# Seven formed heads instead of six in the projections of an attention kernel, with three reorderings of its DMA issues

## What is computed

```python
# attention, 32 heads of 128: INNER = 4096
q = rms_norm(xn @ Wq + bq, gq);  k = rms_norm(xn @ Wk + bk, gk);  v = xn @ Wv + bv
attn = softmax(einsum("bhqd,bhkd->bhqk", q, k) * 128 ** -0.5)
x = x + layernorm(einsum("bhqk,bhkd->bhqd", attn, v) @ Wo + bo)      # xn = layernorm(x)
# feed-forward: a base product, and 8 gated experts of rank 16
x = x + layernorm(xn @ W_base.T + b_base + moe(xn) * 2.0)            # xn = layernorm(x)
```

## Time and profile before

| | |
|---|---|
| plain runs, us | 1054.54 (1053.43 to 1057.06) |
| profiled execution, us | 1056.27 |
| its span, us | 1054.5 |
| TensorE busy | 1034.8 us, 98% |
| VectorE, ScalarE, GpSimd busy | 851.4, 781.6, 769.7 us |
| mean granted clock | 0.995 of full speed |

### The profile page before, as it was taken

One profiled execution on the slowest core, in us unless ns is written; L12 is line 12 of the kernel. 1 busy time (PEld: TensorE's weight loads), 2 busy tenths in 40 slices (PEclk: granted clock), 3 DMA queues, 4 the chain that ended last, 5 costly groups with the idle time before them and its releaser, 6 DMA issues.

```text
span 1054.5 us, 18881 instructions
## 1 busy us (share of the span) xinstructions
PE 1034.8 (98%) x5613; PEld 547.3 (52%) x5613; DVE 851.4 (81%) x1849; ACT 781.6 (74%) x1614; POOL 769.7 (73%) x715
## 2 busy tenths in 40 slices
PE   8999999999999999999999999999999999999997
PEld 5444444444434655556555555555555555555454
DVE  8887888788775788777887887788788788888887
ACT  4775767678876777775788788688787878878656
POOL 2799999977877477775777877778778778767313
PEclk9999999999999999999999999999999999999999
DMA  6789766677674779987777767967876886986812
GB/s 243 198 218 273 246 208 237 193 218 231 201 182 143 199 169 260 246 154 200 160 166 182 196 172 181 193 176 161 217 182 151 210 196 166 228 200 141 175 37 80
DMA packets 312772, 200.04 MB, mean 190 GB/s; under 512 B 275553, under 2 KB 279521, under 8 KB 312673
## 3 DMA queue, kind: packets, MB, share of 16 engines
q1 hardware_dynamic: 304752, 194.24, 71.0%
q10 hardware_dynamic: 7920, 4.62, 2.2%
HBM read 96.03 MB, written 35.68 MB: 125 GB/s over the span
## 4 chain that ended last, share of the span: by engine, by line
PE 88%; DVE 3%; ACT 3%; DMA 3%; issue 2%; POOL 1%; ACTq 0%; SPq 0%; POOLq 0%; DVEq 0%
PE ps L1852 25%; PE ps L1854 25%; PE ps L1853 25%; PE ps L2115 3%; PE ps L2116 3%; PE ps L2117 3%; DMA qk_top_scratch<-qk_top 2%; PE ps L1975 1%; PE ps L1977 1%; PE ps L1976 1%; DVE stats L2419 1%; ACT squares L1260 0%; DMA y<-x 0%; POOL otl L1046 0%; PE ps L2031 0%
## 5 line engine op out<-in xcount | busy, mean ns | idle before, releaser
L2943 DVE SCALAR_TENSOR_TENSOR pair_q<-ps,row_inv,pair_q 128x512 f16<-128x512 f32 x256 | 174.4, 744 | 50.5 <-ACT pair_q L1541 47.3
L1532 ACT ACTIVATE ps<-ps,neg_max 128x512 f32<-128x512 f32 x256 | 168.2, 657 | 51.7 <-DVE ps L2929 51.7
L2929 DVE TENSOR_SCALAR_CACHE_REDUCE ps<-ps,score_down 128x512 f32<-128x512 f32 x256 | 177.3, 756 | 17.4 <-PE ps L1854 16.7
L1541 ACT ACTIVATE pair_q<-ps,row_inv 128x512 f16<-128x512 f32 x256 | 154.4, 689 | 5.7 <-DVE row_inv L2936 5.6
L1852 PE MATMUL ps<-xh,wa_hi 128*128 128x512 f16 x416 | 158.3, 381 | 0.3 <-DVE wa_lo L2535 0.3
L1853 PE MATMUL ps<-xl,wa_hi 128*128 128x512 f16 x416 | 158.1, 380 | 0.0
L1854 PE MATMUL ps<-xh,wa_lo 128*128 128x512 f16 x416 | 158.1, 380 | 0.0
L1013 POOL TENSOR_TENSOR k_lo<-qk_in,k_hi 128x512 f16<-128x512 f32 x62 | 71.7, 1156 | 37.9 <-ACT k_hi L1489 37.8
L1852 PE MATMUL ps<-wo_hi,oth 128*128 128x512 f16 x256 | 97.1, 379 | 1.7 <-issue 0.9
L1852 PE MATMUL ps<-k_hi,qk_in 128*128 128x512 f16 x256 | 97.2, 380 | 1.0 <-issue 0.7
L1854 PE MATMUL ps<-wo_hi,otl 128*128 128x512 f16 x256 | 97.1, 379 | 0.0
(11 more groups left out here) (368 smaller groups left out, 2742.7 us busy)
## 6 DMA issues: line engine op xcount, KB each, us to landing
q_k_scratch<-qk_out SPq DMA_DIRECT2D x64, 512.0 KB, 4.3
qk_in<-q_k_scratch SPq DMA_DIRECT2D x64, 512.0 KB, 3.7
wa_stage<-w_qk SPq DMA_DIRECT2D x32, 512.0 KB, 6.1
u_stage<-w_vo SPq DMA_DIRECT2D x32, 512.0 KB, 7.3
wo_stage<-w_vo SPq DMA_DIRECT2D x16, 512.0 KB, 5.6
x_first<-w_vo SPq DMA_DIRECT2D x12, 512.0 KB, 4.7
qk_tops<-qk_top_scratch ACTq DMA_DIRECT2D x27, 128.0 KB, 5.1
pair_k<-pair_q SPq DMA_TRANSPOSE x130, 4.0
```

Source lines behind the costliest of these rows:

```text
L1532: act.activation(ps[:, SCORE + i, :], ps[:, SCORE + i, :], ACT.Exp, bias=neg_max[:, sl, i:i + 1], scale=-1.0, accum_out=row_sum[:, sl, i:i ...
L1541: act.activation(pair_q[:, 0, i, :], ps[:, SCORE + i, :], ACT.Identity, scale=row_inv[:, sl, i:i + 1]).then_inc(high_ready, 1)
L2929: dve.tensor_scalar(ps[:, SCORE + i, :], ps[:, SCORE + i, :], score_down[:, sl, i:i + 1], None, ALU.mult, ALU.min, accum_out=neg_max[:, sl ...
L2943: dve.scalar_tensor_tensor(out=pair_q[:, 1, i, :], in0=ps[:, SCORE + i, :], scalar=row_inv[:, sl, i:i + 1], in1=pair_q[:, 0, i, :], op0=AL ...
```

## The change

It does four things.
1. `FIRST` becomes 8: the odd head of pair 8 (head 17) is formed as well, seven heads in all. With it the four sums for the first formed head on GpSimd go from ahead of pair 8 to ahead of pair 7.
2. ScalarE's load of the tops for the next even head goes from ahead of the query of batch 1 to behind that query, the second copy into `K_BANK` and the rest of the query.
3. On SyncE the weights and the unit of the next pair's even head are issued ahead of the formed head's two stores.
4. `top_v` is reduced, stored and loaded ahead of and behind pairs 8 and 9, where it was pairs 12 and 13.

```diff
-        FIRST, LAST_PAIR = PAIRS // 2 + 1, PAIRS - 2
+        FIRST, LAST_PAIR = PAIRS // 2, PAIRS - 2
@@ SyncE, formed_pair
-                weights(h)
-                load_unit(h + 3, 1, h + 3)
+                if p == FIRST:
+                    weights(h)
+                    load_unit(h + 3, 1, h + 3)
                 weights(h + 1)
                 store_even(0)
                 if p < LAST_PAIR:
                     load_unit(h + 4, 0, h + 4)
                 store_even(1)
+                if p < LAST_PAIR:
+                    weights(h + 2)
+                    load_unit(h + 5, 1, h + 5)
                 sp.wait_ge(k_out_ready, 2 * h + 4)
                 sp.wait_ge(q_lo_ready, 4 * FIRST + 2 * f + 2)
                 for b in range(2):
                     sp.dma_start(q_k_scratch[h + 1:h + 2, b].rearrange("a p w n -> p (a w) n"),
                                  qk_out[:, 1, b]).then_inc(stored[1][b], 16)
-            for p in range(FIRST, LAST_PAIR - 1):
+            for p in range(FIRST, LAST_PAIR + 1):
                 formed_pair(p)
-            sp.wait_ge(v_top_ready, 1)
-            sp.dma_start(vo_top_scratch[0], top_v[:, :]).then_inc(v_top_stored, 16)
-            formed_pair(LAST_PAIR - 1)
-            sp.wait_ge(v_top_stored, 16)
-            sp.dma_start(tops_v[:, :], vo_top_scratch[0:1].broadcast_to([P, P])).then_inc(v_tops_loaded, 16)
-            formed_pair(LAST_PAIR)
+                if p == FIRST:
+                    sp.wait_ge(v_top_ready, 1)
+                    sp.dma_start(vo_top_scratch[0], top_v[:, :]).then_inc(v_top_stored, 16)
+                if p == FIRST + 1:
+                    sp.wait_ge(v_top_stored, 16)
+                    sp.dma_start(tops_v[:, :], vo_top_scratch[0:1].broadcast_to([P, P])).then_inc(v_tops_loaded, 16)
@@ ScalarE, formed_pair
                 square_key(0, 6)
-                if p < LAST_PAIR:
-                    load_tops(h + 4, 0)
                 act.wait_ge(acc_ready, 4 * h + 4)
                 even_query(1, 7)
                 act.wait_ge(k_out_ready, 2 * h + 2)
                 copy(K_BANK, 8)
                 even_rest(1, 4)
+                if p < LAST_PAIR:
+                    load_tops(h + 4, 0)
@@ VectorE
-            for p in range(FIRST, LAST_PAIR - 1):
-                formed_pair(p)
             largest_value()
-            formed_pair(LAST_PAIR - 1)
-            formed_pair(LAST_PAIR, value_scales)
+            for p in range(FIRST, LAST_PAIR + 1):
+                formed_pair(p, value_scales if p == LAST_PAIR else None)
```

## The result

The changed kernel takes 1059.17 us (median of 22 runs, 1053.28 to 1065.89), the kernel before 1055.91 in the same session (22 runs, 1053.43 to 1061.7). The ratio is 1.0027, 95% interval 1.0016 to 1.0038: 3 us slower, where 1051.0 and a gain were predicted, and outside the range of 1048.4 to 1055.2. The profiled execution took 1061.99 us, with a span of 1060.0 against 1054.5 of before. That is 5.5 us more, so it shows more of the loss than the median has.

The account below looks back on a forecast made before the run. It took TensorE, 98% busy, as the bound, plus a stall in pair 13. From the profiled 1056.27 us it took 1.3 for six matmuls and 4.1 for the stall, added 0.1 for late loads: 1051.0, range 1048.4 to 1055.2.

Parts of the forecast that it names:

- Step 4: Small store of top_v moves to pairs 8/9, its meeting with the tops' store into pair 9: 0, 2.0 us if late.
- the prediction's own deadline: Formed head's stores may land as late as 16.7 us into the next pair, whose formed key wants them.
- Step 2: Load of the tops behind ScalarE's copy: pair 13's stall goes, -4.1 us; the load's lateness costs 0, at most 1 us.
- the cover of 0.3 us: In pair 13 the copy could end at 300.0, against 300.36 when TensorE wants it.
- The stall itself: Before pair 13's last product TensorE stands still 2.36 us, then the slow clock costs 1.7: 4.1 us in all.
- Step 1: Head 17 formed: 48 matmuls of 512 columns become 42 on TensorE, 1.3 us less.
- Step 3: SyncE issues next weights and unit ahead of the formed head's stores, issued no later: 0, bounds -1 and +4 us.
- Step 5: GpSimd's four sums for head 17 ahead of pair 7 make it 3.4 to 4.3 us later: cost 0, at most 3.5.
- The stall moves to pair 9: Rival: the stall goes to pair 9 with the small store; 1053.0 to 1055.1 us, chance 0.14.
- Slower: Rival: formed head's stores land too late in many pairs behind 1 MB of loads; 10 us lost, 1061, chance 0.08.

Follow-up runs that it names:

- e: Changed kernel with the small store of top_v moved inside pair 8, between the even head's two stores; 1054.50 us, ratio 0.9988 to the kernel before.
- i: Kernel before with only the small store of top_v, its load and the reduction moved to around the first formed pairs (9, 10); ratio 1.0023.
- d: Changed kernel with FIRST back at 9, so six formed heads, and the small store behind pair 9; ratio 0.9994 to the kernel before.
- l: Changed kernel with six formed heads and the small store of top_v inside pair 9; ratio 0.9996 to the kernel before.
- f: Kernel before with only ScalarE's load of the tops moved behind the copy of the odd head; ratio 1.0002.
- a: Changed kernel with the small store of top_v, its load and VectorE's reduction back at their old places; ratio 1.0026 to the kernel before.
- o: Kernel before with only the small store of top_v moved into pair 13, between the even head's two stores; ratio 0.9965.
- g: Kernel before with seven formed heads and nothing else changed; ratio 0.9994.
- p: Kernel before with seven formed heads and the small store of top_v moved into pair 13; ratio 0.9966.
- h: Kernel before with only SyncE's next weights and unit issued ahead of the formed head's stores; ratio 0.9993.
- b: Changed kernel with SyncE's old order, the formed head's stores ahead of the next weights and unit; ratio 1.0016 to the kernel before.
- n: Changed kernel with SyncE's old order of stores and loads, and the small store of top_v inside pair 8; ratio 0.9980 to the kernel before.
- q: Changed kernel with the small store inside pair 8, and in pair 8 alone the next loads behind the formed head's stores; ratio 0.9968 to the kernel before.
- m: Changed kernel with the small store of top_v issued twice in a row behind pair 8; ratio 1.0036 to the kernel before.

## Why the prediction was wrong

- **Step 4 failed, and it decides.** "The bad meeting with the store of the tops moves with it, into pair 9. Early pairs lag less ... I take 0." The place was right, the price was not. In pair 9 of the changed kernel's profile the meeting costs 8.4 us of standstill and 1.6 of clock. Moved to a quiet place, the ratio falls from 1.0027 to 0.9988 (e); brought in alone, it is 1.0023 (i). The price also hangs on the seventh head, as d (0.9994) and l (0.9996) show: with six heads and the other parts of the change, the meeting costs plain runs nothing that is told apart.
- The lag of 4.7 us for the stores' issue was taken from pair 10 of before. In the changed kernel it was 8.0 us: GpSimd's low half that gates them ended 7.1 us into the pair (it waited 0.73 us for ScalarE and took 2.31 us for the first half in place of 1.15), and the issues that now stand in front added 0.9. By the prediction's own deadline, 16.7 us into the pair, that leaves 8.7 us for landings of 13. In e, where they go out 6.1 us into the pair, even 10.8 us were too long, and TensorE waited 0.89.
- **Step 2 failed as a sum.** "By this alone the stall goes: -4.1 us." f, with this part alone, measured 1.0002. The copy was in time for the last product of pair 13, as forecast. The term that was left out is the next one: the unit's load, issued behind the small store, landed after 12.1 us, and through VectorE it held the first formed product of pair 14 until 308.32, where it stood before (308.39). The prediction looked only at the key, the copy and the load of the tops, for which it took "0, at most 1 us". In a, where the unit's load has moved ahead, the stores hold pair 13 instead. The key itself was later than it assumed: 14.2 us behind the first formed product of its pair in f, 13.8 before, which used up the cover of 0.3 us, though TensorE did not wait for it there.
- **The stall itself was read right**: it is in plain runs, at about its full size in the session of o, which takes away its cause alone and gains 3.7 us (0.9965), against the 4.1 forecast for it.
- **Step 1 right in the profile, not measurable in the time**: 6 matmuls fewer, pair 8 at 19.4 us in g, ratio 0.9994; o and p do not differ.
- **Step 3 right alone within 0.2% (h, 0.9993), wrong in one point.** That the stores "are issued no later" overlooked that an issue can hold the queue: 3.64 us for one load of weights, of which 0.9 us reached the stores. Taking this part back in the changed kernel gained nothing that is told apart (b, 1.0016). Pairs 10 and 11 of the changed kernel keep 19.4 us with the loads in front.
- **Step 5: the four sums were sized right, the cost of being behind was not.** They took 3.3 us, but what followed slowed down too. GpSimd's timeline of the changed kernel in pairs 7 and 8, and then an instruction of VectorE:

```profile
174.21 1.26 POOL L907 TENSOR_TENSOR w_sum<-wa_stage 128x512 f32<-128x512 f32 x1
175.44 2.09 POOL L912 TENSOR_TENSOR w_sum<-wa_stage 128x256 f32<-128x256 f32 x3
...
181.51 2.42 POOL L823 TENSOR_TENSOR qk_out<-q_s,qk_out 128x512 f16<-128x512 f32 x1
...
192.12 3.41 POOL L832 TENSOR_TENSOR acc<-acc,squares 128x512 f32<-128x512 f32 x2
195.51 1.15 POOL L849 TENSOR_TENSOR xs<-qk_in,xs 128x512 f16<-128x512 f32 x1
```

```profile
180.35 2.56 DVE L2551 SCALAR_TENSOR_TENSOR w_form_a<-w_sum,qk_up,w_form_a 128x1280 f16<-128x1280 f32 x1
```

  The last form of x starts 11.1 us into pair 8, where the earlier trace rows has 188.45 - 183.8 = 4.7: 6.5 us later, not 3.4 to 4.3. An instruction of 1.15 us took 2.42 beside VectorE's of 2.56, which took 1.54 at 205.33. The Trainium skill's rule on the shared port ("SBUF — State Buffer", Who interferes with whom) agrees in kind, and the prediction applied it to the four sums and not to what they push into VectorE's work. ScalarE's key square waited 1.43 us for it. In g a backlog of the same sums alone costs TensorE nothing; how much of the formed head's late stores comes of it in company is not shown.
- **The rivals.** Two were half right. "The stall moves to pair 9" had the place and priced it by the old standstill. "Slower" had the mechanism, stores that land later than the room left for them, and spread it over many pairs where it struck one. Put together they were what happened. They got 0.22 between them as separate cases, and nothing as one.

What stays open: why the formed head's stores of pair 8 land in 9 to 11 us in e, n and q and in 4.6 in g; why the meeting costs plain runs 0.23% in i and nothing in d, both with six heads; and whether the parts lose more together than apart. The plain runs of d against the changed kernel speak for it, the sum of the four parts alone does not decide it.

## What to carry to other kernels

When a stall ends with a late DMA, look for the transfer that makes its neighbours late before moving the instruction that waits: moving the wait uncovered the next one (f, 1.0002), moving the 0.5 KB store to a stretch without large stores removed them both (o, 0.9965). For each new place of such a transfer ask what is under way there and how late that may land, and count no slack that is smaller than the spread of the landings in the trace.

## What the runs showed of the hardware

- 128 pieces of 4 bytes, issued among stores and loads of 512 KB, were followed by 11 to 28 packets of 4096 bytes that took 2 to 6.5 us each instead of 0.159. With the pieces moved away the same places had none (e, o, p). Twice as many pieces did no more harm that could be told apart (m). Batches of slow packets also come without them, up to 25 within 18 us, with none over 4.7 us in the stretches shown.
- An issue of a 512 KB load of weights on SyncE's queue took 0.42 us as a rule, and 3.64 us at 207.93 in the changed kernel, right behind the issue of a store.
- A GpSimd difference of two 128x512 inputs took 1.15 us, and 2.42 beside a VectorE instruction with two inputs that itself took 2.56 instead of 1.54.
